# A DLRM tower on one core: the last selected pair of units 2 and 3 is gathered, and the gathers' spacing is changed

## What is computed

```python
e = jnp.stack([tbl_0[ids[:, 0]], ..., tbl_31[ids[:, 31]]], axis=1)
gram = jnp.einsum('bnd,bmd->bnm', e, e)
z = gram[:, rows, cols]          # rows < cols
h = jnp.concatenate([z, dense_ctx], axis=1)
h = jnp.maximum(h @ W_top1 + b_top1, 0.0)      # 512 x 512
h = jnp.maximum(h @ W_top2 + b_top2, 0.0)      # 512 x 256
y = h @ W_top3                                 # 256 x 1
```

## Time and profile before

| | us |
|---|---|
| median of 3 runs | 417.81 |
| lowest and highest | 417.23, 419.79 |
| the profiled execution | 418.46 |
| its span, first to last instruction | 416.66 |
| PE busy in it | 376.1 |
| POOL busy in it | 276.0 |
| DVE busy in it | 229.8 |
| ACT busy in it | 165.5 |

### The profile page before, as it was taken

One profiled execution on the slowest core, in us unless ns is written; L12 is line 12 of the kernel. 1 busy time (PEld: TensorE's weight loads), 2 busy tenths in 40 slices (PEclk: granted clock), 3 DMA queues, 4 the chain that ended last, 5 costly groups with the idle time before them and its releaser, 6 DMA issues.

```text
span 416.7 us, 15183 instructions
## 1 busy us (share of the span) xinstructions
PE 376.1 (90%) x6576; PEld 214.2 (51%) x6576; DVE 229.8 (55%) x717; ACT 165.5 (40%) x264; POOL 276.0 (66%) x746
## 2 busy tenths in 40 slices
PE   0668787998989999999999999999999999989897
PEld 0334333455555554566455555565545555555586
DVE  2999999964647886007168887007258983000000
ACT  4346766622116935230354435230364425331222
POOL 6888888864447888655587898756488988610000
PEclk9999999999999999999999999999999999999999
DMA  5954751110103785101176821110077311015710
GB/s 169 381 144 139 255 175 43 44 43 17 19 17 62 152 217 194 23 16 19 19 140 153 236 69 47 23 21 17 14 132 151 74 20 24 19 19 95 148 49 0
DMA packets 38266, 37.51 MB, mean 90 GB/s; under 512 B 13804, under 2 KB 26936, under 8 KB 38072
## 3 DMA queue, kind: packets, MB, share of 16 engines
q1 hardware_dynamic: 29576, 28.54, 26.8%
q0 software_dynamic: 6144, 6.30, 7.4%
q10 hardware_dynamic: 2480, 1.71, 1.4%
HBM read 28.45 MB, written 8.09 MB: 88 GB/s over the span
## 4 chain that ended last, share of the span: by engine, by line
PE 75%; DVE 16%; ACT 3%; DMA 2%; issue 2%; ACTq 1%; DVEq 0%
PE sel_ps L523 38%; PE tower_ps L569 13%; DVE onehot L468 11%; PE gram_ps L554 10%; PE tower_ps L579 6%; PE gat_ps L539 3%; PE tower_ps L523 3%; PE gat_ps L523 3%; DVE tabs L456 2%; DVE work L451 2%; ACT vecs L334 2%; DMA ids_wide<-ids_scratch 1%; DMA ids_scratch<-sel_f 1%; DMA sel_ids<-in_ids_sel_dram 1%; ACTq L180 1%
## 5 line engine op out<-in xcount | busy, mean ns | idle before, releaser
L468 DVE TENSOR_SCALAR onehot<-ids_wide,row_ids 128x512 bf16<-128x512 f16 x688 | 201.2, 364 | 97.7 <-PE sel_ps L523 85.1
L297 POOL DMA_INDIRECT rows<-in_tbl_dram,gat_ids x192 | 195.4, 1018 | 71.4 <-PE gram_ps L554 52.3
L523 PE MATMUL sel_ps<-onehot,tabs 128*64 128x512 bf16 x1872 | 211.6, 382 | 29.7 <-DVE onehot L468 17.5
L523 PEld LDWEIGHTS sel_ps<-onehot,tabs 128*64 128x64 bf16 x1872 | 110.5, 110 | 124.5 <-issue 28.4
L334 ACT COPY vecs<-sel_ps 64x256 f32<-64x256 f32 x144 | 87.3, 606 | 91.8 <-PE sel_ps L523 73.3
L293 POOL MEMSET spare<- 128x1 f32 x546 | 80.5, 147 | 20.4
L569 PE MATMUL tower_ps<-work,w_sb 128*128 128x512 f32 (+1 forms) x160 | 58.7, 515 | 1.0 <-ACT h L357 1.0
L554 PEld LDWEIGHTS gram_ps<-vecs 64*32 64x32 f32 x4096 | 38.6, 105 | 26.6 <-issue 26.4
L554 PE MATMUL gram_ps<-vecs 64*32 64x32 f32 x4096 | 43.2, 201 | 5.9 <-issue 5.8
L569 PEld LDWEIGHTS tower_ps<-work,w_sb 128*128 128x128 f32 x160 | 29.2, 190 | 20.8 <-issue 17.2
L475 DVE COPY work<-gram_ps 128x512 f32<-128x512 f32 x8 | 5.2, 687 | 53.6 <-PE gram_ps L554 53.6
(11 more groups left out here) (19 smaller groups left out, 56.3 us busy)
## 6 DMA issues: line engine op xcount, KB each, us to landing
ids_wide<-ids_scratch SPq DMA_DIRECT2D x40, 256.0 KB, 5.7
rows<-in_tbl_dram,gat_ids POOLq DMA_INDIRECT x192, 2.5
products<-work SPq DMA_DIRECT2D x12, 248.0 KB
products<-work SPq DMA_DIRECT2D x24, 120.0 KB
work<-in_packed_dram SPq DMA_DIRECT2D x5, 512.0 KB, 5.4
work<-products SPq DMA_DIRECT2D x9, 256.0 KB
work<-in_packed_dram SPq DMA_DIRECT2D x3, 640.0 KB, 4.1
work<-in_packed_dram ACTq DMA_DIRECT2D x2, 512.0 KB, 5.0
```

The costliest lines, as they stand in the source:

```text
L297: nc.gpsimd.indirect_dma_start(out=rows[:, r, k, h, :], out_offset=None, in_=tables[GATHERED[k]], in_offset=bass.IndirectOffsetOnAxis(ap=g ...
L468: last = nc.vector.tensor_scalar(onehot[:, n % RING, c - c0, :], ids_wide[:, k, :], row_ids[chunks[k]][:, c:c + 1], None, ALU.is_equal)
L523: last[at] = nc.tensor.matmul(sel_bank(u, g)[DIM * at:DIM * at + DIM, :], tabs[:, first_chunk[k] + c, part, :], onehot[:, piece_no(u, g, h ...
```

## The change

In units 2 and 3 (MORE), pair 9, that is fields 30 and 31 with ten chunks each, is no longer selected. Its two fields are gathered instead: a fourth turn, of two fields, in each round, and 56 gathers a unit in place of 48, 208 in all. In these units the turns of round 0 follow pairs 5, 6, 7 and 8. A spacer is now a fill and a wait for that same fill, so the gather behind it waits too; there are two after each gather of unit 0 and one after every other. BEHIND is renumbered, and in round 0 of unit 3 it lets three gathers pass per gate where it let two, with a fourth gate at chunk (3, 0, 3).

```diff
+MORE = (2, 3)
+GAT_FIELDS = GATHERED + SELECTED[-2:]
+N_ROWS = len(GAT_FIELDS)
...
-NEAR_SPACERS, SPACERS = 1, 3
-NEAR_SPACED = range(48, 63)
-
-BEHIND = {48: (0, 0, 0), 50: (0, 0, 1), 52: (0, 0, 2), 54: (0, 0, 3),
...
-          187: (3, 0, 0), 189: (3, 0, 1), 191: (3, 0, 2)}
+FIRST_SPACERS, SPACERS = 2, 1
+
+BEHIND = {50: (0, 0, 0), 52: (0, 0, 1), 54: (0, 0, 2), 56: (0, 0, 3),
...
+          144: (2, 0, 0), 146: (2, 0, 1), 148: (2, 0, 2), 150: (2, 0, 3),
+          156: (2, 1, 0), 157: (2, 1, 1), 159: (2, 1, 2), 160: (2, 1, 3),
+          196: (3, 0, 0), 199: (3, 0, 1), 202: (3, 0, 2), 205: (3, 0, 3)}
+
+
+def pairs(u):
+    return N_PAIRS - 1 if u in MORE else N_PAIRS
+
+
+def groups(u):
+    return GROUPS + [range(N_GAT, N_ROWS)] if u in MORE else GROUPS
+
+
+def turns(u):
+    return len(groups(u))
...
             def spacer():
-                n = next(count)
-                if n > 0:
-                    pool.wait_ge(spaced, n)
                 nc.gpsimd.memset(spare[:], 0.0).then_inc(spaced, 1)
+                pool.wait_ge(spaced, next(count) + 1)
...
-                    if u > 0 and k == GROUPS[x].start and h == 0:
+                    if u > 0 and x < turns(u - 1) and k == groups(u)[x].start and h == 0:
                         pool.wait_ge(gat_full, gat_no(u - 1, r, x) + 1)
-                    if len(of_unit) * u + n in BEHIND:
-                        chunk_done(*BEHIND[len(of_unit) * u + n])
+                    if first + n in BEHIND:
+                        chunk_done(*BEHIND[first + n])
                     gather(u, r, x, k, h)
-                    for _ in range(NEAR_SPACERS if len(of_unit) * u + n in NEAR_SPACED else SPACERS):
+                    for _ in range(FIRST_SPACERS if u == 0 else SPACERS):
                         spacer()
...
             for u in range(UNITS):
-                for g in range(6 if u == 1 else 2, N_PAIRS):
+                for g in range(6 if u == 1 else 2, pairs(u)):
                     select(u, g)
                     if g == 2 and u > 1:
                         layer3(u - 2)
-                    if g >= N_PAIRS - N_TURNS:
-                        turn(u, 0, g - N_PAIRS + N_TURNS)
+                    if g >= pairs(u) - turns(u):
+                        turn(u, 0, g - pairs(u) + turns(u))
```

More of the change, by code:

```diff
@@ L41 @@
 MOVES = 3 * Q
-NEAR_SPACERS, SPACERS = 1, 3
-NEAR_SPACED = range(48, 63)
-BEHIND = {48: (0, 0, 0), 50: (0, 0, 1), 52: (0, 0, 2), 54: (0, 0, 3),
[6 rows of a table removed]
+FIRST_SPACERS, SPACERS = 2, 1
+BEHIND = {50: (0, 0, 0), 52: (0, 0, 1), 54: (0, 0, 2), 56: (0, 0, 3),
[6 rows of a table added]
+def pairs(u):
[4 more added lines that the diff above has]
+    return len(groups(u))
 def sel_no(u, g):
-    return N_PAIRS * u + g
+    return sum(pairs(v) for v in range(u)) + g
 def gat_no(u, r, x):
-    return N_TURNS * (ROUNDS * u + r) + x
+    return ROUNDS * sum(turns(v) for v in range(u)) + turns(u) * r + x
 def emptied_no(u, r, b):
@@ L67, in piece_no @@
 def piece_no(u, g, half, at):
-    return 4 * (N_PAIRS * u + g) + 2 * half + at
+    return 4 * sel_no(u, g) + 2 * half + at
 def pair_row(n, m):
@@ L253, in _ @@
             for u in range(LAST):
-                for w in range(N_PAIRS):
+                for w in range(pairs(u + 1)):
                     load_wide(u + 1, w)
@@ L391, in _ @@
             for u in range(UNITS):
-                for g in range(2, N_PAIRS):
+                for g in range(2, pairs(u)):
                     selected(u, g)
@@ L398, in _ @@
                         middle(g + 4)
-                    if g >= N_PAIRS - N_TURNS:
-                        gathered(u, 0, g - N_PAIRS + N_TURNS)
+                    if g >= pairs(u) - turns(u):
+                        gathered(u, 0, g - pairs(u) + turns(u))
                 if u == 0:
@@ L410, in _ @@
                 if u == 0:
-                    for x in range(N_TURNS):
+                    for x in range(turns(u)):
                         gathered(u, 1, x)
@@ L492, in _ @@
             for u in range(1, UNITS):
-                for g in range(N_PAIRS):
+                for g in range(pairs(u)):
                     one_hots(u, g, 0)
@@ L536, in turn @@
                     pe.wait_ge(gat_emptied, n - 1)
-                pe.wait_ge(rows_in[r][x], 16 * 2 * len(GROUPS[x]) * (u + 1))
-                for at, k in enumerate(GROUPS[x]):
+                pe.wait_ge(rows_in[r][x], 16 * 2 * len(groups(u)[x]) * sum(x < turns(v) for v in range(u + 1)))
+                for at, k in enumerate(groups(u)[x]):
                     last = nc.tensor.transpose(gat_ps[:, n % 2, P * at:P * at + P],
@@ L632, in _ @@
                     select(u + 1, 0)
-                    for x in range(2, N_TURNS):
+                    for x in range(2, turns(u)):
                         turn(u, 1, x)
```

32 lines of the change are left out of this document (17 added, 15 removed), and 8 rows, old and new, of the table BEHIND.

## The result

The changed kernel takes 413.1 us (412.88 to 413.97, 4 runs), beside it the kernel before took 418.59: ratio 0.987, interval 0.984 to 0.991. That is faster, by 5.5 us or 1.3 per cent, and clear of the interval; predicted were 10.3. It lies 0.1 above the upper end of the range (404.3 to 413.0). A repetition on another chip (run 10) gave 414.38 against 418.71, which is 4.3. One execution of run 1 (419.38 us, with a mean granted clock of 0.944) was in a slower state of the chip and is left out of that run's median. The profiled execution took 413.97 us, its span 412.2; against the profiled execution of before (418.46) that is -4.49.

The account below looks back on a forecast made before the run. PE was taken to bound the kernel, without a break from 73.20 us on. The terms -13.2 - 0.2 - 1.0 + 0.9 + 3.2 sum to -10.3, from 417.81 to 407.5 us; range 404.3 to 413.0.

Parts of the forecast that it names:

- The removal: Pair 9 in units 2 and 3: 2 x 60 matmuls leave the PE chain, 2 x 6.60 = 13.2 us saved.
- the 0.5 waits for one-hots: Between pairs 6 and 7 in units 2 and 3: a turn covers PE's wait for DVE, -1.0 us in all.
- The spacing: POOL's gathers with one awaited fill: pitch 1.33 us in quiet stretches, 1.40 beside one-hots; unit 0 left at 0.
- POOL in time: Free stretches before units 2 and 3: with 36 gathers POOL reaches the gates only about 1 us late.
- POOL becomes the bound: Rival: pitch stays near 1.73 us, PE waits for rows in units 2 and 3, 426.5 us; chance 0.04.
- Denser gathers slow DVE: Rival: were each added gather to cost DVE double, about 0.9 us per unit shows, 410 us; chance 0.13.
- The -0.2 on chunk (1, 0, 0): Unit 1's first gram chunk: without unit 2's last ids load over it, 0.2 us saved.
- The wait that is added: Turn (3, 1, 3): PE waits for the last gathers' rows, so gram (3, 1, 0) starts later, +3.2 us, bounds +2.8 to +4.3.
- SP's transfers of round 0 are done in the meantime: During the wait before round 1 of unit 3: given as a reason that nothing hides the +3.2 us.
- it is in the old time already: Gram chunks under late gathers: cost 0.56 us once, nothing another time, so nothing was added.
- The clock rival: Rival: clock falls to 1.2 GHz in the new idle stretch and stays for grams and layer 2, +15, 423 us; chance 0.03.
- a PEclk below 1: Sign that the forecast is wrong: PE's clock below the 2.4 GHz level, 1.00 in every window taken before.

Follow-up runs that it names:

- run 10: The unmodified change, measured again on another chip beside its shifted form and two other variants: 414.38 us, ratio 0.986 to the kernel before.
- run 1: The change with four gathers per gap in round 0 of unit 3 and no gate at chunk (3, 0, 3): 409.27 us, ratio 0.976 to the kernel before.
- run 5: The change with its gates but the old spacing, three fills with the last not awaited, after every gather: 423.73 us, ratio 1.011 to the kernel before.
- run 6: The kernel before with only the new spacing and its old gates: 418.45 us, ratio 0.9993 to the kernel before.
- run 3: The change with PE doing the first output of layer2(2) ahead of turn (3, 1, 3), no work added: 414.27 us, ratio 0.988 to the kernel before.
- run 4: The change with the first half of layer2(2)'s first output computed three times, twice before the last turn: 411.88 us, ratio 0.982 to the kernel before.
- run 2: The change without any gate in unit 3: 409.15 us, ratio 0.978 to the kernel before.
- run 7: The change with three gathers per gap also in round 0 of units 1 and 2, two gates in unit 3: 408.14 us, ratio 0.974 to the kernel before.
- run 8: The kernel of run 7 with 32 small matmuls in unit 0, shifting PE's code by half a block: 405.19 us, ratio 0.968 to the kernel before.

## Why the prediction was half right

**Right.** The removal: two pairs of 6.60, and the 0.5 waits for one-hots, which are gone from units 2 and 3. (1, 1, 3) to (2, 0, 0) lost 6.56 (56.53 to 49.97) and (2, 1, 3) to (3, 0, 0) 6.71 (57.03 to 50.32), against 6.6 + 0.5 - 0.3 = 6.8 for each. The spacing: 1.33 was taken and is 1.33 (339.22 to 340.55); beside one-hots 1.36 to 1.45. POOL in time: no wait of PE for rows in unit 2. The rival "POOL becomes the bound" had a right condition, as run 5 shows. "Denser gathers slow DVE" did not come (run 6: ratio 0.9993). But POOL was later at its gates than the 0.6 and 0.9 us that were worked out: gather 144 started at 257.59, 2.2 behind the chunk's end at 255.41, gather 196 at 346.89, 1.7 behind 345.19; in the free stretch POOL beside one-hots was at 1.45 more often than at 1.36, and it stood once in each stretch, for 1.4 and 1.3 us, on "issue". The -0.2 on chunk (1, 0, 0) came, but for another reason than the load of ids: that chunk took 1.52 in run 5, which has not that load, and 1.29 in run 6, which has it. Before, and in run 5, a gather starts 0.01 us behind its start. That was luck.

**Wrong in size: "The wait that is added", +3.2.** That wait was there, once, in the turn that was named, and from (3, 0, 3)'s start to (3, 1, 0)'s it made 9.58 us out of 4.33, +5.25. Its terms, as taken and as measured: the gate's release 0.28, now 0.78 (360.48 to 361.26), since the gather waits for a gate and for its fill (run 6, which changes the spacing alone, has 0.79 at its gate of 207.75); two pitches of 1.33, right; the landing 2.5, now 3.45, beside SP's stores of the products that run from 361.62 on (DMA share 0.63 in 361 to 367, where it was 0.07 before); from landing to gram 0.8, now 1.30, of which 0.25 is the clock (the two transposes took 0.66, in run 1 at full clock 0.41). The last 0.1 is a gather in chunk (3, 0, 3). The landing was inside the bounds that I gave (up to 3.6), the sum was not (+4.3). "SP's transfers of round 0 are done in the meantime" was the wrong sentence: beside them the last three gathers took 3.59, 3.21 and 3.45 to land, in runs 3 and 4 2.96 to 3.59, while the last four of run 1, of which only the last lands beside stores, took 2.38 to 2.73. A landing of 3.49 (gather at 354.02) occurs without stores too, so that the stores are the cause is likely, not shown.

**Wrong at a price: "it is in the old time already".** I had the one chunk at 1.85 in the rows and a gather 0.58 us ahead of another that cost nothing, and did not ask at which offset a gather costs. Unit 2's first chunk had paid before, unit 3's had not. The tighter pitch and three gathers to a gap put a gather into or at the start of all four chunks of unit 3's first round: 1.82, 1.83, 1.40 and 1.39 against 4 x 1.29, which is +1.3 (0.1 of it is counted in the wait above), and 0.2 in unit 2's second chunk.

**The clock rival happened, and cost little.** I gave it 0.03 and +15 us, though a PEclk below 1 stood among the signs of being wrong. It fell in the wait of the last turn and stayed for 10.24 us. The first four matmuls of layer 2 took 3.78 where four take 1.98, and the step from (3, 1, 0) to (3, 1, 1) 5.18 where it took 3.12 before; the next took 3.28 for 3.77, and all behind it as long as before. But the part behind (3, 1, 0) took 41.53 us with the fall and 41.68 in run 2, 42.06 in run 7, with a short one or none: there PE waits for its code within the chunks (1.6 in run 2, 1.59 and 1.30 in run 7). So what the fall cost net is not separated from what code would have cost without it; run 4 puts it at 0 to 1.9 us. The rule of the Trainium skill (TensorE: Matmul & The Clock Gate, "Part 1: The HAM clock gate") on an idle engine was the better guide than the short gaps of the earlier trace rows.

**Not in the sum at all: code loading.** That PE takes as long as before where its work is the same was the silent assumption in unit 0 and behind (3, 1, 0). A pair 9 less is 60 matmuls and 60 weight loads, 120 instructions or nearly half a block, and moves the ends of all later blocks. The kernel before had the "issue" waits in its own trace (3.5 us from 100 to 130 us), and no row of the prediction looks there. In unit 2 it gave +1.24. In unit 0 the code ahead is the same and only the moments differ: the -1.31 is within the 3 us by which single executions differ there, and the second execution of the change had +1.67 in its place. The last part's +1.54 is clock and code together: runs 1, 2, 7 and 8 and their repetitions, without the long wait, had 40.9 to 42.3 there, before had 39.99.

Together, the stretches of the table: the wait +2.05, gathers in chunks 1.2 in unit 3 and 0.2 in unit 2, code +1.24 in unit 2, unit 0's -1.31 and the start's +0.54, which are scatter, the last part +1.54, and 0.44 in unit 1's stretch, where the first gram chunk gave its 0.2 back (1.50 to 1.29), chunk (1, 1, 1) took as much (1.29 to 1.49), and the selection behind lost 6.56 and not 6.8. That is +5.8, from -10.3 to -4.5. That the profiled execution comes out at -4.5 owes 1.3 us to unit 0's luck; in the execution of run 10 the span was 414.1, only 2.5 under before.

## What to carry to other kernels

Before a long row of small instructions (a gram chunk has 256 in 1.3 us), look for "issue" waits inside groups and at the instruction queue: what is removed far ahead of them shifts the blocks of code, and this can give or take 3 us where no other view shows a change. When a gate is moved later, work out release, landing and copy with the traffic of the new moment, not with the medians of the old trace, and ask what PE's clock does in the wait. A DMA issued by POOL isn't free for PE: place it beside long matmuls (a pair of 6.60 us did not grow), not within small ones (a chunk of 1.29 grew to 1.82).

## What the runs showed of the hardware that I had not expected

- A gather that POOL starts 0.45 to 0.88 us into a gram chunk makes the chunk 0.53 us longer (1.29 to 1.82), one that starts just ahead of it 0.1 to 0.2.
- PE's code comes in 16 KB packets, one each 3.6 us in unit 0's gram stage. A wait for code ends 1.2 to 1.6 us after a packet's end (47 cases) and takes up to 2.7 us, in run 3.
- A gather behind a gate and an awaited fill starts 0.78 us after the gram's end, behind a gate alone 0.28.
- With the clock at 0.50 for 10 us, a stage that otherwise waits for its code took no longer (41.53 against 41.68 and 42.06).
- The same kernel took 410.58 us on one chip and 511.99 on another, with the kernel before at 418.7 and 420.2 beside it. No run explains it.
